# A graph-attention kernel: when GpSimd may begin to fetch a group's edge rows

## What is computed

```
xn = layernorm(x);  xp = xn + xn @ Wpos + bpos + deg * Wdeg + bdeg
q, k, v = xp @ Wq + bq, xp @ Wk + bk, xp @ Wv + bv          # 8 heads of 16
att   = clip(sum_over_head(q[dst] * k[src]) / 4, -50, 50)     # nan becomes 0
alpha = softmax of att over the edges of one dst
x = x + segment_sum(v[src] * alpha, dst) @ Wo + bo
x = x + gelu(layernorm(x) @ W1 + b1) @ W2 + b2
```

## Time and profile before

| | |
|---|---|
| device time, median of three runs | 2097.13 us |
| the profiled execution, span from first to last instruction | 3221.0 us |
| TensorE busy / VectorE busy / GpSimd busy in it | 1677.5 / 1445.7 / 1486.6 us |
| indirect DMAs issued by GpSimd | 1564 (782 a layer) |
| mean granted TensorE clock | 0.694 |

### The profile page before, as it was taken

How to read it: one execution, slowest core, us unless ns; L and a number is a source line. 1 busy time by engine, 2 the same in 40 slices (tenths; PEclk the granted TensorE clock), 3 DMA queues, 4 the chain that set the end, 5 groups by cost and what they waited for, 6 DMA issues and landing times.

```text
span 3221.0 us, 44116 instructions
## 1 busy us (share of the span) xinstructions
PE 1677.5 (52%) x11693; PEld 1432.5 (44%) x11694; DVE 1445.7 (45%) x2484; ACT 910.1 (28%) x1616; POOL 1486.6 (46%) x1584
## 2 busy tenths in 40 slices
PE   7444444355566556555343534444456565556545
PEld 5344334345455445444333433343445454545444
DVE  8634434344444535454363434343444444434435
ACT  3212212123333323332131212122233233323322
POOL 0545444545444444544534445444544444444452
PEclk9667676767666777775666767676677667666667
DMA  2423333323323333333323333233333333333332
GB/s 74 136 85 109 95 99 97 105 93 113 97 95 105 108 99 96 114 105 97 116 72 101 102 95 107 90 102 98 102 103 104 103 93 98 110 98 99 101 119 75
DMA packets 120301, 322.97 MB, mean 100 GB/s; under 512 B 31459, under 2 KB 43684, under 8 KB 120170
## 3 DMA queue, kind: packets, MB, share of 16 engines
q0 software_dynamic: 75072, 205.10, 21.5%
q1 hardware_dynamic: 44292, 115.07, 10.7%
q10 hardware_dynamic: 838, 1.60, 0.2%
HBM read 313.45 MB, written 9.73 MB: 100 GB/s over the span
## 4 chain that ended last, share of the span: by engine, by line
another core or an unknown queue 29%; DVE 21%; issue 20%; PE 15%; DVEq 11%; ACT 2%; ACTq 0%; DMA 0%; POOL 0%; POOLq 0%
PE ps L1352 8%; DVE dots L1082 5%; DVEq L359 4%; PE ps L1337 4%; DVE msg L1106 4%; DVE prod L1072 3%; DVEq L393 2%; DVE hot L992 1%; DVEq L992 1%; DVE acc L987 1%; PE ps L1314 1%; DVEq L987 1%; DVE not_nan L1084 1%; DVE q_parts L839 1%
## 5 line engine op out<-in xcount | busy, mean ns | idle before, releaser
L566 POOL DMA_INDIRECT kv<-kv_tab,src_idx x1564 | 1482.8, 948 | 1697.8 <-DVE msg L1106 1131.3
L1352 PE MATMUL ps<-msg,hot 128*128 128x136 f32 x3896 | 783.3, 366 | 766.4 <-DVE acc L987 459.0
L1352 PEld LDWEIGHTS ps<-msg,hot 128*128 128x128 f32 x3896 | 705.0, 264 | 827.5 <-issue 531.8
L1337 PE MATMUL ps<-q_parts,hotT 128*128 x5844 | 545.4, 251 | 608.3 <-issue 436.6
L1337 PEld LDWEIGHTS ps<-q_parts,hotT 128*128 x5844 | 449.5, 113 | 717.5 <-issue 700.3
L1072 DVE TENSOR_TENSOR prod<-kv,ps 128x1024 f32<-128x1024 f32 (+1 forms) x198 | 238.1, 1202 | 608.3 <-remote 431.3
L705 ACT ACTIVATE hotT<-dist 128x1024 bf16 x246 | 259.9, 1057 | 535.0 <-remote 388.1
L992 DVE SCALAR_TENSOR_TENSOR hot<-dst_col,neg_base,ps 128x1024 f32<-128x1024 f32 (+1 forms) x246 | 311.8, 1267 | 144.4 <-issue 141.0
L702 ACT ACTIVATE dist<-dst_rows,neg_node 128x1024 bf16<-128x1024 int32 x246 | 282.4, 1148 | 146.1 <-issue 135.5
L987 DVE TENSOR_TENSOR acc<-acc,ps 128x136 f32 x246 | 71.3, 290 | 553.7 <-remote 316.1
L1082 DVE TENSOR_REDUCE dots<-prod 128x64 f32<-128x1024 f32 (+1 forms) x198 | 238.8, 1206 | 33.3 <-DVE prod L1072 24.2
(11 more groups left out here) (215 smaller groups left out, 995.4 us busy)
## 6 DMA issues: line engine op xcount, KB each, us to landing
dst_rows<-in_dst SPq DMA_DIRECT2D x194, 512.0 KB
kv<-kv_tab,src_idx POOLq DMA_INDIRECT x1564
kv_tab<-qkv SPq DMA_DIRECT2D x25, 128.0 KB
kv_tab<-qkv SPq DMA_DIRECT2D x3, 768.0 KB, 3.8
out_tab<-z SPq DMA_DIRECT2D x24, 64.0 KB
out<-out_tab SPq DMA_DIRECT2D x1, 1498.5 KB, 7.2
hot<-in_L_gnn_W SPq DMA_DIRECT2D x2, 256.0 KB
w<-in_L_gnn_W SPq DMA_DIRECT2D x2, 256.0 KB
```

Source lines behind the costliest of these rows:

```text
L566: pool.indirect_dma_start(kv[:, u, c, :], None, kv_tab[l][:, :], bass.IndirectOffsetOnAxis(ap=src_idx[:, c, at(g)], axis=0)).then_inc(kv_i ...
L1337: last = MM(qd[:, c * P:(c + 1) * P], hotT[:, bass.ds(pr % 2, 1), c * P:(c + 1) * P], q_parts[:, at(t), k * D:(k + 1) * D], start=first an ...
L1352: last = MM(agg, hot[:, u % 2, c, :], msg[:, u % 2, c, :], start=(c == 0), stop=(c == nch - 1))
```

## The change

GpSimd's wait ahead of a group is another one from the ninth group of a layer on (g >= 8). It no longer asks that the messages of group g - 4 are done, but that TensorE has done the first product of the query gather of group g - 1. TensorE raises a new semaphore `q_begun` at that product, once a group. Groups 4 to 7 keep the old wait. Because a query gather of group g - 1 waits for `prod_done` of group g - 2, and VectorE writes the messages of g - 4 ahead of that, the new wait includes the old one. To have semaphores left for it, three pairs of old ones are merged: two for the transposed index rows, two of the tail's projections, and the copy of the output now counts on `tab_out`.

```
-        src_T = sem("src_T")
-        dst_T = sem("dst_T")
+        rows_T = sem("rows_T")
...
+        q_begun = sems("q_begun")
...
-        out_copied = sem("out_copied")
-        tail_kv_ps = sem("tail_kv_ps")
-        tail_q_ps = sem("tail_q_ps")
+        tail_ps = sem("tail_ps")
...
-                    sp.dma_start(out_d[P:N, :], out_tab[P:N, :]).then_inc(out_copied, 16)
+                    sp.dma_start(out_d[P:N, :], out_tab[P:N, :]).then_inc(tab_out, 16)
...
-                    sp.wait_ge(out_copied, 16)
+                    sp.wait_ge(tab_out, 16 * NU + 16)
...
                     if g >= SLOTS:
-                        pool.wait_ge(msg_done[l], g - SLOTS + 1)
+                        if g < 2 * SLOTS:
+                            pool.wait_ge(msg_done[l], g - SLOTS + 1)
+                        else:
+                            pool.wait_ge(q_begun[l], g)
...
-            act.wait_ge(src_T, 1)
+            act.wait_ge(rows_T, 1)
...
-            act.wait_ge(dst_T, 1)
+            act.wait_ge(rows_T, 2)
...
                                 last = MM(qd[:, c * P:(c + 1) * P], hotT[:, bass.ds(pr % 2, 1), c * P:(c + 1) * P],
                                           q_parts[:, at(t), k * D:(k + 1) * D], start=first and c % 4 == 0 and k == 0,
                                           stop=True, skip_group_check=True)
+                                if first and c == 0 and k == 0:
+                                    last.then_inc(q_begun[l], 1)
...
-                    MM(in_tail["kv"], z2T[0], wfold[:, l + 1, D:3 * D], start=True, stop=True).then_inc(tail_kv_ps, 1)
-                    MM(in_tail["q"], z2T[0], wfold[:, l + 1, 0:D], start=True, stop=True).then_inc(tail_q_ps, 1)
+                    MM(in_tail["kv"], z2T[0], wfold[:, l + 1, D:3 * D], start=True, stop=True).then_inc(tail_ps, 1)
+                    MM(in_tail["q"], z2T[0], wfold[:, l + 1, 0:D], start=True, stop=True).then_inc(tail_ps, 1)
```

More of the change, by code:

```diff
@@ L1168, in _ @@
                 if l < L - 1:
-                    for ready, banked, done, a, b in ((tail_kv_ps, in_tail["kv"], next_done, D, 3 * D),
-                                                      (tail_q_ps, in_tail["q"], tail_q_done, 0, D)):
-                        dve.wait_ge(ready, 1)
+                    for ready, banked, done, a, b in ((1, in_tail["kv"], next_done, D, 3 * D),
+                                                      (2, in_tail["q"], tail_q_done, 0, D)):
+                        dve.wait_ge(tail_ps, ready)
                         if a:
@@ L1197, in row_transposes @@
                 pe.wait_ge(consts, NCONST)
-                for which, bank, done in ((src_f, 0, src_T), (dst_f, 2, dst_T)):
+                for which, bank in ((src_f, 0), (dst_f, 2)):
                     for c in range(GC):
                         last = MM(ps[:, bank + c // 4, (c % 4) * NG:(c % 4 + 1) * NG], which[:, c * P:(c + 1) * P], mirror[:, :], start=True, stop=True)
-                    last.then_inc(done, 1)
+                    last.then_inc(rows_T, 1)
             def pair_sums():
```

## The result

| | before | after |
|---|---|---|
| median, us | 2097.24 (2096.16 to 2097.57, 6 runs) | 2105.47 (2102.96 to 2109.52, 6 runs) |
| ratio, 95% interval | | 1.0045 (1.0035 to 1.0055) |

The change costs 8.2 us, 0.4%: slower by more than the 0.2% that can be told. That is inside the range, but not what I thought likeliest.

The account below looks back on a forecast made before the run. GpSimd issuing gathers every 1.25 us was taken as the bound: 87.0 + 977.5 + 25.5 + 977.5 + 24.5 = 2092.0 us, against 2097.1 measured. Forecast: 2097.1 + 0 + 0 + about 1 = 2098 us, range 2070 to 2140.

Parts of the forecast that it names:

- The bound: Without the profiler GpSimd issues gathers with no gap worth naming, 10.0 us a full group; everything else hides under it.
- The sum of 2092.0: GpSimd's time: start 87.0, two layers' gathers at 977.5 each, 25.5 between them, 24.5 at the end.
- I take them for something that comes with recording: Halts of VectorE, TensorE and ScalarE, some 15 us each, 99 of them, were put down to the profiler.
- Merged semaphores and signal: 0: Merged semaphores outside the loop and 198 increments on TensorE's products were to add 0 us to the time.
- The bound of 43 us: Upper limit for the signal's cost on TensorE: 198 increments at one product's 0.22 us each.
- The place of the edge: Slot stage, odd groups: projections and feed-forward delay TensorE's query gather to 6.2 us after the product, leaving least slack.
- The size of the slack: GpSimd's spare time before the new event: 5.1 us in plain groups, 4.1 in even and 0.7 in odd slot-stage groups.
- rival B: Odd slot-stage groups after two-pair groups make GpSimd wait: 18 x 0.9 = 16 us, 2113 us; chance 0.35.
- Groups after a tile border, "about 1": Forecast's allowance of about 1 us in all for the few groups after a tile border.
- The signs: Expected in the changed profile: wait named TensorE, bursts under 16 gathers, spacing 1.25, product to query gather 1.8, 2.8, 6.2 us.
- Rival C: Engines halt in every run during GpSimd's bursts; the new wait shortens halts, an eighth of 477 us less, 2037; chance 0.13.
- Rival D: Halts in every run; two groups' lead is too short, four more halts of 15.77 us make 2160 or more; chance 0.10.

Follow-up runs that it names:

- without waits: Profiled execution of the changed kernel with an earlier event in groups 37 to 84 and the old wait in groups 8 to 15; median 2098.26 us.
- both places eased: Changed kernel, but groups 37 to 84 wait for VectorE's product of group g - 2 and groups 8 to 15 keep the old wait; 2098.26 us, ratio 1.0001.
- pauses between gathers: Changed kernel with the old wait everywhere and a 0.22 us memset, waited for, behind each gather; 2663.06 us, ratio 0.8407 on a 3180 chip.
- the later event: Changed kernel with the signal at the 23rd of 24 query-gather products, not the first; 2681.55 us (0.8410) on a 3180 chip, 2118.22 us (1.0086) on a 2097 chip.

## Why the prediction was right and wrong

- *The bound.* Right on the chip that was asked for. The sum of 2092.0 stands against a span of 2096.1 without waits. The gathers take 6.3 us more than the sum has, nearly all of it the spacing, 1.254 us instead of 1.25 (1065.78 - 85.99 over 781 gathers), and start and end 2.2 us less. The Trainium skill's advice in Perfetto Trace Analysis (GPSIMD Engine Instruction) to go by the spacing of starts is borne out: by the 948 ns of the rows the sum was 477 us short, and what fills it is no wait but 0.30 us of "issue" before each gather, 472.6 us in all.
- *"I take them for something that comes with recording."* Wrong. On a 3180 chip the time is there with and without recording (3168.73 us recorded, 3168.95 to 3202.42 in the other runs, for the change without its wait), and a recorded execution on the other kind takes what an unrecorded one takes (2108.91 us beside 2102.96 to 2109.52). The profile of before is most likely from a chip of the other kind: it has 60 long bursts and a wait for messages of 1131.3 us, as the change without its wait has there (60, and 1076.4 us). Which chip it was taken on is not known, and its span of 3221.0 us lies a little above every run timed on that kind (up to 3202.42). Read so, the sum over GpSimd was a forecast for a chip whose profile I had not seen, and it held there. The count of the halts was rough as well: not 99 of some 15 us, but 37 waits "remote" of 11.7 us in the mean in the earlier trace rows, and 60 bursts.
- *Merged semaphores and signal: 0.* Right. On a 2097 chip, where GpSimd is the bound, the run with both places eased has them all and gives 1.0001; the run with the whole change but its wait gives 0.9999, on a 3180 chip. The bound of 43 us was far off.
- *The place of the edge.* Right: VectorE's product to TensorE's next query gather, in odd groups of the slot stage. Moving the event from the second to the first of these in that stage alone gave back 4.9 us.
- *The size of the slack.* This is the step that failed: "I expect the slack to hold, mostly". The range holds the result, but by way of rival B; the forecast's own 2092 to 2102 doesn't. Three terms were off. The landing is 1.9 to 2.0 us (layer 1's group 92: issued by 2034.1, product at 2036.1) and not 3.1; the Trainium skill's fixed cost of about 2.0 us (DMA: Bandwidth & Descriptors, Anatomy of one DMA), which I had set aside for the row, agrees with it. The row's 3.0 us came from the end of a halt. The odd query gather comes 5.0 us after its product in the median, 7.85 us at most, and not 6.2. Both were too dear, so an odd group of median length has 3.0 us to spare, if VectorE is on time, and not 0.7. The third was too cheap: I let VectorE be 1.0 to 1.3 us late, for groups with two pairs. It is up to 4.9 us late beyond the landing (group 62: 6.8), because lateness carries over. Groups 59 to 61 took it 13.0, 9.1 and 12.6 us, against 10.0 for GpSimd. In 46 of the 96 slot-stage groups the product begins more than 3 us after the last gather. So the 0.7 us came near the edge by errors that partly cancelled: which groups cross it is decided by the lateness.
- *Rival B's price.* The mechanism was right, its 16 us were twice too much. Not 18 groups lose 0.9 us each: five lose 0.8 to 2.2 us, 7.1 us in all (8.6 us of waits less 0.30 each). Ahead of each of the five stands a group with two pairs, as B has it, one to three groups before the late one; but most of the 18 such groups cost nothing. So B had too many groups, each too cheap.
- *Groups after a tile border, "about 1".* Nothing was to be seen of them. What I had no term for is the start of layer 0, where VectorE begins 26 us behind GpSimd and has not caught up by group 8: 2.4 us. The run that eased that place as well went from 3.3 to 0.6 us over the kernel before. Nor had I a term for the end of layer 1, where the output copy meets group 95's rows and group 97 has half the gathers: 3.1 us in the changed kernel's profile and 1.4 in one other, nothing in three. The old wait, four groups back, does not ask for anything so late.
- *The signs.* The wait is named TensorE, as said, but only ten times. "Bursts of fewer than 16" is wrong here: the event is mostly early, and up to 440 gathers follow each other without a gap. The way from product to next query gather is 1.9 us in the median of the plain and of the even groups; 2.8 us is the longest of the even ones.
- *Rival C* is what happens on the 3180 chips: the halts are in every run and the new wait shortens them, by 10% and not by an eighth of 477 us. I gave it little because the sum over GpSimd left no room for halts; on the chip that was asked for there are none. *Rival D*, that a short lead is fatal, holds on neither kind: on a 3180 chip VectorE is halted more often, as it says, but for less long.

What sets off the halts, and why two kinds of chip differ, stays open. TensorE's mean granted clock is lower on the 3180 chips too (0.701 for the change without its wait, 0.829 for the changed kernel on a 2097 chip). That alone does not make the halts: they are idle time, and VectorE's busy time is the same in the earlier trace rows and in the changed kernel's page (1445.7 and 1452.9 us). Whether the lower clock follows from the halts is not shown. What is shown is that the spacing of the gathers is not touched by them, that in the stretches looked at the other engines come back some 2 to 3 us after the last gather of a burst, and that each of two edits, pauses between gathers and the later event, takes 16% off the time.

No version beats both kernels everywhere. On 2097 chips the best of the changed ones equals the kernel before. On 3180 chips the pauses (0.8407) and the later event (0.8410) are level at the top. On the others the pauses were not tried; 1564 gathers at 1.45 us are 2268 us, more than the whole kernel takes, by my estimate.

## What to carry to other kernels

When an engine is saturated, replace the event that it waits for only by one that comes early enough in the *worst* group, and count that group with the lateness it inherits from its neighbours, not with its own time alone. Look at the ends as well: the first groups, where the consumer starts behind, and the last, where a short group gives less lead and other transfers may be in the way. A wait that asks for work far back, even if it looks loose, is what lets two engines of uneven pace run free of each other. And if a profile's span is far from the time that was measured, ask whether both come from the same kind of chip before blaming the recording.

## What the runs showed of the hardware that I had not expected

- The same program takes 2097 us on two chips (and in the comparison) and 3180 us on two others, each steady, within 0.2% and 1.6%. The spacing of the gathers is 1.25 us on both; it is TensorE, VectorE and ScalarE that stand still or trickle while GpSimd issues.
- On the second kind, a memset of 0.22 us behind each of 1564 gathers, with a wait for it, makes the kernel 516 us faster.
- Halving the size of the gathered rows, 153 to 104 GB/s over the whole kernel, left the gather's 0.95 us and the spacing as they were; the rows were there 0.2 us sooner.
- One copy of 1498.5 KB on SyncE's queue goes with rows that land 4.8 to 8.0 us after the last gather of their group instead of 1.9 to 2.0 (1.7 for half rows).
- A late wait repairs itself in part: GpSimd's wait of 2.54 us took 2.2 us off the distance between gather and product.
